# A fused decoder block on Trainium2: column halves and a narrow inverse root in the first cross-attention

## What is computed

```python
q = einsum('oc,bcn->bon', Wq, x);  k, v = split(einsum('oc,bcn->bon', Wkv, context), 2)
q = softmax(split_heads(q), axis=-2) * scale     # over the 64 channels of a head
k = softmax(split_heads(k), axis=-1)             # over the 512 positions
ctx = einsum('bhdn,bhen->bhde', k, v)
out = einsum('bhde,bhdn->bhen', ctx, q)
out = einsum('oc,bcn->bon', Wout, out) + b_out
return (out - mean(out, 1)) * rsqrt(var(out, 1) + 1e-05) * g
x = layernorm(x + <that>)
```

## Time and profile before

| | us |
|---|---|
| median of 3 runs | 2332.91 |
| lowest, highest | 2332.28, 2333.55 |
| the profiled execution's own time | 2332.89 |
| its span, first to last instruction | 2331.0 |
| PE busy in the span | 2224.3 (95%) |
| DVE busy | 1300.0 (56%) |
| ACT busy | 781.4 (34%) |
| POOL busy | 772.1 (33%) |
| xattn0 on PE, first projection to first product of ffn0 | 563.20 to 859.81 |

### The profile page before, as it was taken

How to read it: one execution, slowest core, us unless ns; L and a number is a source line. 1 busy time by engine, 2 the same in 40 slices (tenths; PEclk the granted TensorE clock), 3 DMA queues, 4 the chain that set the end, 5 groups by cost and what they waited for, 6 DMA issues and landing times.

```text
span 2331.0 us, 33907 instructions
## 1 busy us (share of the span) xinstructions
PE 2224.3 (95%) x11762; PEld 1769.8 (76%) x11762; DVE 1300.0 (56%) x2151; ACT 781.4 (34%) x1475; POOL 772.1 (33%) x709
## 2 busy tenths in 40 slices
PE   8999999997999989999899999999989999999978
PEld 6888888885555547887788888888878888887867
DVE  3454444447677733334345444444766767766766
ACT  2233222223677742222233232222333333232321
POOL 4222222202343336344422122221454344434233
PEclk9999999999999999999899999999999999999989
DMA  4212221221000032230222332222222222222120
GB/s 165 72 58 79 81 79 51 68 55 47 12 17 18 14 126 95 86 108 0 86 72 65 82 82 73 55 73 55 70 65 68 61 61 81 63 72 54 32 78 37
DMA packets 120545, 152.41 MB, mean 65 GB/s; under 512 B 16272, under 2 KB 67984, under 8 KB 119952
## 3 DMA queue, kind: packets, MB, share of 16 engines
q1 hardware_dynamic: 120464, 151.33, 22.4%
HBM read 124.02 MB, written 27.26 MB: 65 GB/s over the span
## 4 chain that ended last, share of the span: by engine, by line
PE 80%; issue 7%; DVE 7%; POOL 4%; ACT 2%; DMA 0%; POOLq 0%; DVEq 0%; ACTq 0%; SPq 0%
PE banks L283 20%; PE banks L285 19%; PE banks L284 18%; PE banks L598 7%; PE banks L641 3%; PE banks L1279 3%; PE banks L1263 2%; POOL f_wl L1690 1%; PE banks L1245 1%; PE banks L1252 1%; PE banks L1215 1%; PE banks L1231 1%; POOL f_il L1698 1%; DVE st L351 1%; PE banks L1269 1%
## 5 line engine op out<-in xcount | busy, mean ns | idle before, releaser
L283 PE MATMUL banks<-xTh,wh 128*128 128x512 f32 x1024 | 418.5, 409 | 11.7 <-DVE xTl L1965 7.5
L285 PE MATMUL banks<-xTh,wl 128*128 128x512 f32 x1024 | 404.3, 395 | 0.0
L284 PE MATMUL banks<-xTl,wh 128*128 128x512 f32 x1024 | 403.2, 394 | 0.0
L283 PE MATMUL banks<-woh,oth 128*128 128x512 f32 x768 | 313.5, 408 | 16.3 <-DVE X L936 7.0
L284 PE MATMUL banks<-wol,oth 128*128 128x512 f32 x768 | 301.8, 393 | 0.0
L285 PE MATMUL banks<-woh,otl 128*128 128x512 f32 x768 | 301.7, 393 | 0.0
L1031 POOL TENSOR_TENSOR sc_sb<-sc_sb,rs 128x512 f32<-128x512 f32 x96 | 103.7, 1083 | 553.2 <-DVE rs L890 553.2
L936 DVE TENSOR_TENSOR X<-banks,X 128x512 f32<-128x512 f32 x192 | 132.0, 688 | 272.9 <-PE banks L285 272.0
L733 ACT ACTIVATE q_sb<-banks 128x512 f32<-128x512 f32 x192 | 114.6, 597 | 402.0 <-PE banks L285 402.0
L283 PEld LDWEIGHTS banks<-xTh,wh 128*128 128x128 f32 x1024 | 195.2, 191 | 52.5 <-issue 9.3
L285 PEld LDWEIGHTS banks<-xTh,wl 128*128 128x128 f32 x1024 | 194.6, 190 | 43.6
(11 more groups left out here) (214 smaller groups left out, 4010.6 us busy)
## 6 DMA issues: line engine op xcount, KB each, us to landing
raw<-in_a_in SPq DMA_DIRECT2D x144, 256.0 KB, 2.8
raw<-in_a_out SPq DMA_DIRECT2D x96, 256.0 KB, 2.8
turned<-pq SPq DMA_DIRECT2D x384, 64.0 KB, 1.8
pt<-turned SPq DMA_DIRECT2D x96, 256.0 KB, 2.8
f_q<-in_f_q SPq DMA_DIRECT2D x21, 512.0 KB, 3.8
f_s<-in_f_s SPq DMA_DIRECT2D x21, 512.0 KB, 5.3
X<-in_x SPq DMA_DIRECT2D x1, 2048.0 KB, 10.7
x_craw<-in_ctx SPq DMA_DIRECT2D x8, 256.0 KB, 2.7
```

The lines of the kernel that those rows point to most:

```text
L283: nc.tensor.matmul(out, w_hi, x_hi, start=start, stop=False)
L284: nc.tensor.matmul(out, w_hi, x_lo, start=False, stop=False)
L285: return nc.tensor.matmul(out, w_lo, x_hi, start=False, stop=stop)
```

## The change

In words:

- `G0` does both batches: 8 products, batch b into partitions 64b to 64b+63 of bank `gm`, that is with weights in column half b of the array, the two batches alternating. `G1` is gone; one `gt` of 128x512 takes the place of two of 64x512. `M0` and `M1` read rows 0 to 63 and 64 to 127 of `x_gt` and of `x_u`, which the setup computes for both halves (16 products for 8). `M1` waits for `m0`.
- `x_m` has no zeros any more: 64 columns per batch. `OUT0` does both batches, 8 products of 128x64 weights, batch b into partitions 64b on, alternating. `OUT1` and the zeroing of `x_m` are gone.
- `VAR` has the squares as weights and two columns of `x_blk` as the moving operand: 4 products of 128x128 by 2 columns, whose 8 results per partition lie in bank `out`. DVE adds epsilon (`ve`, 128x8), POOL raises to -1/2 (`pw`, 128x8), and `BR` on PE spreads the result back over 128x512 of bank `out`: 8 products with 64 equal weight columns and the identity, 128 columns, moving, in column halves. `y` reads that bank. `ln`, `rd` and their two table loads are gone.
- The high part of the context (`ch` on ACT) becomes `chi` on POOL.
- All four orders are new. `OUT` now waits for `y` of the tile before.
- PE's first half of ffn0 stands behind the last `BR`; ACT's high parts stand behind `qc7` and `oc` of tile 7. POOL's hook is the same text, behind `cp` of tile 6.

```diff
-            x_u = sb("x_u", [64, XH * S])
+            x_u = sb("x_u", [P, XH * S])
...
-            x_gt = sb("x_gt", [64, 2, 512])
-            x_m = sb("x_m", [P, 4, 2, P])
+            x_gt = sb("x_gt", [P, 512])
+            x_m = sb("x_m", [P, 4, 2, S])
-            x_sd = sb("x_sd", [P, DM])
-            x_rd = sb("x_rd", [P, DM])
+            x_ve = sb("x_ve", [P, 8])
+            x_r8 = sb("x_r8", [P, 8])
...
-        X_PE = x_order("QT0' K3' KT2' M1'' Q3' KT3' QT1' OUT1'' KT4' XT''' QT2' KT5' Q0 QT3' KT6' VAR'' K0 KT7' "
-                     "QT4' Q1 G0' Q2 QT5' M0' KT0 K1 QT6' G1' QT7' KT1 K2 OUT0' ")
-        X_DVE = x_order("qs0' kn0' qm1' kz'' qs1' y''' m0'' kn1' sm0' bn''' qm2' kn2' xn''' qs2' sm1' kn3' m1'' "
-                     "qm3' qs3' sm2' sm3' xl''' qm0 ")
-        X_ACT = x_order("gt1'' qe1' kc1' qc7'' ke4' ke5' qe2' qc0' kc2' ke6' ke7' ch xhi kc3' qe3' qc1' kc4' "
-                     "xh''' qc2' kc5' sq'' qc3' kc6' ln'' qc4' oc'' kc7' rd'' gt0' ke0 ke1 qc5' qe0 qc6' ke2 "
-                     "kc0 ke3 ")
-        X_POOL = x_order("xl2 cl en4' en5' en6' en7' r'' en0 rs'' en1 en2 cp'' en3 ")
+        X_PE = x_order("Q2' KT2' OUT0'' KT3' K3' QT0' Q3' KT4' QT1' VAR'' XT''' KT5' QT2' Q0 KT6' QT3' K0 KT7' "
+                     "QT4' Q1 G0' QT5' KT0 K1 M0' QT6' BR'' KT1 M1' QT7' K2 ")
+        X_DVE = x_order("sm1' y''' m1'' kn2' qm2' qs2' bn''' sm2' kn3' xn''' qm3' qs3' xl''' ve'' qm0 qs0 kn0 kz' "
+                     "sm3' qm1 sm0 qs1 kn1 m0' ")
+        X_ACT = x_order("ke1 gt0' qc5' kc0 qe1 qc6' ke2 ke3 kc1 qc7' kc2 ke4 ke5 qe2 oc' sq' kc3 qc0 xhi+ ke6 kc4 "
+                     "qc1 xh'' kc5 qc2 ke7 kc6 qc3 qe3 kc7 qe0+ qc4 ke0+ ")
+        X_POOL = x_order("en7' en0 en1 r'' cp''' en2 rs'' en3 chi+ xl2+ cl+ en4 en5 pw' en6 ")
...
-                last = nc.tensor.matmul(pb[h % 2][0:64, (h // 2) * S:(h // 2 + 1) * S], x_wv[r0:r0 + 64, h // 2, :],
-                                        x_woc[r0:r0 + 64, h // 2, :], start=True, stop=True)
+                for c0 in (0, 64):
+                    last = nc.tensor.matmul(pb[h % 2][c0:c0 + 64, (h // 2) * S:(h // 2 + 1) * S],
+                                            x_wv[r0:r0 + 64, h // 2, :], x_woc[r0:r0 + 64, h // 2, :], start=True, stop=True)
...
                 elif kind == "G":
-                    wait(pe, xs["ekt"], 8 * q + 7 + u)
-                    wait(pe, xs[f"ctin{u}"], 16 * (q + 1))
+                    wait(pe, xs["ekt"], 8 * q + 8)
+                    for b in range(2):
+                        wait(pe, xs[f"ctin{b}"], 16 * (q + 1))
+                    wait(pe, xt_ready, q - 1)
+                    for n in range(4):
+                        for b in range(2):
+                            last = nc.tensor.matmul(XB["gm"][64 * b:64 * b + 64, :], x_ct[:, b, n, :], x_ekT[:, b, n, :],
+                                                    start=n == 0, stop=n == 3)
+                    last.then_inc(xs["g"], 1)
+                elif kind == "M":
                     if u == 0:
-                        wait(pe, xs["sd"], q)
+                        wait(pe, xs["gt"], q + 1)
                     else:
                         wait(pe, xs["mr"], 2 * q + 1)
+                    r = slice(64 * u, 64 * u + 64)
                     for n in range(4):
-                        last = nc.tensor.matmul(XB["gm"][0:64, :], x_ct[:, u, n, :], x_ekT[:, u, n, :],
-                                                start=n == 0, stop=n == 3)
-                    last.then_inc(xs["g"], 1)
-                elif kind == "M":
-                    wait(pe, xs["gt"], 2 * q + u + 1)
-                    for n in range(4):
-                        last = nc.tensor.matmul(XB["gm"][:, n * P:(n + 1) * P], x_gt[0:64, u, n * P:(n + 1) * P],
-                                                x_u[0:64, n * P:(n + 1) * P], start=True, stop=True)
+                        last = nc.tensor.matmul(XB["gm"][:, n * P:(n + 1) * P], x_gt[r, n * P:(n + 1) * P],
+                                                x_u[r, n * P:(n + 1) * P], start=True, stop=True)
                     last.then_inc(xs["m"], 1)
                 elif kind == "OUT":
-                    wait(pe, xs["mr"], 2 * q + u + 1)
-                    wait(pe, xs["qcp"], 8 * q + 7 + u)
-                    if u == 0:
-                        wait(pe, xs["osq"], q)
-                        wait(pe, xs["oc"], q)
+                    wait(pe, xs["mr"], 2 * q + 2)
+                    wait(pe, xs["qcp"], 8 * q + 8)
+                    wait(pe, xs["y"], q)
                     for n in range(4):
-                        last = nc.tensor.matmul(XB["out"][:, :], x_m[:, n, u, :], x_q[:, u, n, :],
-                                                start=(u == 0 and n == 0), stop=(u == 1 and n == 3))
+                        for b in range(2):
+                            last = nc.tensor.matmul(XB["out"][64 * b:64 * b + 64, :], x_m[:, n, b, :], x_q[:, b, n, :],
+                                                    start=n == 0, stop=n == 3)
                     last.then_inc(xs["out"], 1)
                 elif kind == "VAR":
                     wait(pe, xs["osq"], q + 1)
-                    wait(pe, xs["mr"], 2 * q + 2)
-                    wait(pe, xt_ready, q)
-                    nc.tensor.matmul(XB["gm"][:, :], x_blk[:, :], x_sq[:, :], start=True, stop=True).then_inc(xs["var"], 1)
+                    wait(pe, xs["oc"], q + 1)
+                    for n in range(4):
+                        last = nc.tensor.matmul(XB["out"][:, 2 * n:2 * n + 2], x_sq[:, n * P:(n + 1) * P],
+                                                x_blk[:, :].rearrange("p (b s) -> p b s", b=2)[:, :, 0], start=True, stop=True)
+                    last.then_inc(xs["var"], 1)
+                elif kind == "BR":
+                    wait(pe, xs["pw"], q + 1)
+                    for n in range(4):
+                        for b in range(2):
+                            last = nc.tensor.matmul(XB["out"][64 * b:64 * b + 64, n * P:(n + 1) * P],
+                                                    x_r8[:, 2 * n + b:2 * n + b + 1].to_broadcast([P, S]), ident[:, :],
+                                                    start=True, stop=True)
+                    last.then_inc(xs["br"], 1)
...
-                if kind == "VAR" and q == NT - 1:
+                if kind == "BR" and q == NT - 1:
                     pe_ffn0(pe, True)
...
-                if kind == "ch" and not (isinstance(q, int) and q == 0):
-                    wait(act, xs["cin"], 16 * (q + 1))
-                    wait(act, xs["k"], 8 * q)
-                    nc.scalar.activation(x_ch[:, :], x_craw[:, :], ACT.Copy).then_inc(xs["chi"], 1)
...
                 elif kind == "gt":
-                    wait(act, xs["g"], 2 * q + u + 1)
-                    wait(act, xs["m"], 2 * (q - 1) + u + 1)
-                    nc.scalar.activation(x_gt[0:64, u, :], XB["gm"][0:64, :], ACT.Copy).then_inc(xs["gt"], 1)
+                    wait(act, xs["g"], q + 1)
+                    wait(act, xs["m"], 2 * q)
+                    nc.scalar.activation(x_gt[:, :], XB["gm"][:, :], ACT.Copy).then_inc(xs["gt"], 1)
...
-                elif kind == "ln":
-                    wait(act, xs["var"], q + 1)
-                    wait(act, xs["rd"], q)
-                    nc.scalar.activation(x_sd[:, :], XB["gm"][:, :], ACT.Ln, bias=x_eps[:, 0:1]).then_inc(xs["sd"], 1)
-                elif kind == "rd":
-                    wait(act, xs["sd"], q + 1)
-                    wait(act, xs["y"], q)
-                    nc.scalar.activation(x_rd[:, :], x_sd[:, :], ACT.Exp, scale=-0.5).then_inc(xs["rd"], 1)
...
-                if kind == "gt" and u == 1 and q == NT - 1:
+                if kind == "qc" and u == 7 and q == NT - 1:
                     high_weight(act, 0, 0)
                     high_weight(act, 0, 1)
-                elif kind == "rd" and q == NT - 1:
+                elif kind == "oc" and q == NT - 1:
                     high_weight(act, 0, 2)
...
-                    wait(dve, xs["out"], 2 * (q - 1) + u + 1)
+                    wait(dve, xs["out"], q)
                     bank = XB["gm"][:, :].rearrange("p (h o) -> p h o", h=4)
                     for h in range(2):
                         r = slice(64 * h, 64 * h + 64)
                         last = nc.vector.scalar_tensor_tensor(
-                            x_m[r, :, u, 64 * u:64 * u + 64], bank[r, :, 64 * h:64 * h + 64], XD ** -0.5,
+                            x_m[r, :, u, :], bank[r, :, 64 * h:64 * h + 64], XD ** -0.5,
                             x_krz[r, 4 * u:4 * u + 4].rearrange("p (h o) -> p h o", o=1).to_broadcast([64, 4, S]),
                             ALU.mult, ALU.mult)
                     last.then_inc(xs["mr"], 1)
+                elif kind == "ve":
+                    wait(dve, xs["var"], q + 1)
+                    wait(dve, xs["pw"], q)
```

(16 more changed lines are left out.)

30 lines of the change are left out of this document (13 added, 17 removed).

## The result

The changed kernel takes **2281.56 us** (median; 2280.18 to 2284.13) beside 2333.23 for the kernel before: ratio 0.9779, with a 95% interval from 0.9762 to 0.9796. That is 51.7 us less; the prediction said 36.5 less. The median lies 0.4 under the low end of the range of 2282 to 2313, and two of the four runs lie inside it. The profiled execution took 2280.18, its span 2278.4. The stage is read from the first query product of xattn0 to the transposes of tile 7, the last thing that ffn0's second half waits for: 307.94 us before (563.20 to 871.14), 257.03 after (561.62 to 818.65), so 50.9 of the 52.7 between the two profiled executions. Of the rest, 1.6 is attn0, which the change does not touch and whose end lies between 560.8 and 564.9 in the runs of this case.

The account below looks back on a forecast made before the run. PE's work was taken to bound the stage. Six periods 30.4, the seventh 5.9 and the start 3, less 0.3 for the setup and 2.5 for the end, gave 36.5 off 2332.9: 2296 us, range 2282 to 2313.

Parts of the forecast that it names:

- Rival A: In `G` and `OUT`, column halves don't run side by side, PE's tile is 34.8: 2347 us, slower; chance 5%.
- Rival B: On PE, weight loads of one half can't run beside the other's products, 4.4 a tile: 2331 us; chance 3%.
- PE per tile, 27.3: In xattn0, PE's work per tile falls from 33.06 to 27.3 us by new prices of `G`, `OUT`, `VAR`, `BR`.
- The period of 28.0: One tile in mid-stage of xattn0 takes 28.0 us instead of 33.06, range 27.3 to 29.5.
- I add 0.7: In the mid-stage period, 0.7 us on PE's 27.3, as PE and DVE with equal turns don't both stay full.
- my round: Walk once round the new order from `qm0`: DVE's waits sum to 2.4 us, its turn to 27.2, as long as PE's.
- case D: In xattn0, overlap is full and the walks have slack: period 27.3, start 6 less, end level, 2286 us; chance 15%.
- `K1` ahead of `Q2`: 3 less: At the stage's start, DVE's wait of 4.39 for `K1` shrinks by the new order: 3 us less, between 0 and 6.
- The seventh period, 5.9: The seventh tile of xattn0, without a next tile's projections, goes from 31.85 to about 26 us: 5.9 less.
- 2.5 more than before: From `G` of tile 7 to ffn0, new work and PE's lower clock make 31.3 us instead of 28.8.
- Rival C: In mid-stage, hand-overs between PE and DVE bind: period 30.5 instead of 28.0, 20 us less gain, 2314 us; chance 12%.
- Five activations: ACT loses five activations (`ln`, `rd`, `ch`, one `gt`) of 0.6 to 0.7 us, besides two table loads of 1.28.

Follow-up runs that it names:

- e7: Changed kernel with both batches' `G` and `OUT` products in one column half, one after the other, the second batch added into the first's place: 2335.9 us, ratio 1.0013.
- e2: Changed kernel with the variance as one 128x512 product and its root by two ACT functions, without `ve`, `pw` and `BR`: 2282.06 us, ratio 0.9791.
- e5: Changed kernel with, in tile 0 alone, the third query pair again ahead of the fourth unit's key transposes and `K1`: 2287.15 us, ratio 0.9801.
- e3: Changed kernel with ffn0's first two low weight parts on POOL behind `rs` of tile 6 instead of `cp`: 2277.94 us, ratio 0.9768.
- e6: As e2, with ACT's second root function behind the last key copies, `y` behind both `M` copies, low parts as in e3: 2270.78 us, ratio 0.9736.
- e11: As e10, with tile 7's variance ahead of tile 6's transposes, `rd` between query copies, `x_xn` ahead of later scalings and `f_wl`: 2272.03 us, ratio 0.9731.
- e10: As e6, with drain orders of its own on PE, DVE and ACT, and ffn0's later scalings spread over tile 6's layer norm: 2276.48 us, ratio 0.9762.
- e12: As e6, another drain: ffn0's first unit behind tile 7's variance, its second behind tile 6's transposes, ACT, DVE and POOL reordered: 2267.42 us, ratio 0.9722.

## Why the prediction was right or wrong

**What bounds the stage, and that the halves run side by side: right.** The forecast rested on `G` and `OUT` falling from 7.16 and 7.07 to 3.7 each. They measured 3.59 and 3.58, and e7 shows that nothing else makes the difference. Rival A (no overlap) falls with it. e7 comes near to what it described and took 2336 instead of the 2347 that I gave it: A priced `BR` at 1.8, while e7 keeps `BR` in column halves at 1.02, and it had the start at 3 instead of 8.5. Rival B falls too: loads of one half are hidden beside products of the other. By the rule of the Trainium skill ("TensorE: Matmul & The Clock Gate", Part 3, The mechanism), a weight load overlaps a running product only if its row group differs. The trace disagrees: with all of the rows in use by both halves, 16 records with 16 loads take 3.59, 0.224 each, while a load alone is 0.14 and a record 0.43 to 0.45.

**PE per tile, 27.3: right within 0.4.** `G` 3.59, `OUT` 3.58, `VAR` 0.82, `BR` 1.02 sum with the old rest to 26.9, as the window shows (26.93). Each of the four prices was 0.08 to 0.12 too high. `BR` at 1.02 lay between its two bounds, 0.6 and 1.8.

**The period of 28.0: wrong, and the largest part of the miss.** The step that failed is "I add 0.7": two engines with equal turns that don't both stay full. In my round DVE's turn came out at 27.2, as long as PE's. Measured, DVE was busy 24.35 and its waits fitted into the 2.6 that were left, so that PE waited for nothing in the middle of the stage. Each wait on the walk was one of DVE, for PE or for ACT, and none was one of PE; a wait of the other engine costs PE nothing as long as the next thing that PE needs is ready. The chance that I should have read from my own walk is case D. e2 shows the other case: 0.29 and 0.62 of waits of PE for ACT and 0.20 for DVE, and there the period was 1.1 over PE's sum. What counts is which engine does the waiting. The miss of 1.07 a period, 0.7 for this term and 0.37 for the prices, is 6.4 us in six; 1.0 more came from the first period, which is 25.9.

**The start: right cause, size too small.** "`K1` ahead of `Q2`: 3 less" measured 3.6 by e5, by the very wait that was named. But the start lost 8.5. The failed step is a term of the sum that was too small: nothing but this one wait was in it. What the new DVE order does in tile 0 besides (its last softmax goes behind the first `G`) was left out, and so was PE's granted clock there, 0.73 before and 0.82 after. Which of them makes the other 4.9 stays open. The range of 0 to 6 was too narrow by it.

**The seventh period, 5.9, and the setup: right.** Measured 5.8. The setup's 32 records take 0.62, as its 16 did: they run in column halves beside each other and cost nothing, instead of 0.3.

**The end: mechanism right in its links, size nearly.** Predicted were `pw` at 1.65 (1.65), an idle PE of 5.8 behind the last `BR` ended by `f_wl` (5.04, `f_wl`), and 2.5 more than before. Up to ffn0's first product it became 0.9 shorter (27.97 against 28.83), and 2.1 of the lower clock fell into ffn0's first half, 13.46 instead of 11.33; both together 1.3 longer. e3 confirms the named culprit: with the low parts one POOL step earlier the stage is 5.8 shorter.

**The range.** 36.5 became 51.7: 7.5 from the periods, 5.5 from the start, 1.2 from the end, 0.3 from the setup, the rest attn0 and what the runs differ by. Rival D named the first of these, and gave 2286; with the start as it measured, it gives 2283. The low end of 2282 was D with a little room for the prices. The period fell under D's, the start by more than D allowed, and the end alone was worse than D's "level"; together they passed the low end by 0.4 us.

**Slips that changed nothing.** Rival C's own sum, 2296 and 8 x 2.5, gives 2316 and not 2314. "Five activations" less on ACT are four, as its own list has them, and the measured 5.2 us less is what two table loads and four activations make. The chain before is not of PE products alone: at 626 us it has one copy by ACT, a wait of 0.40.

## What to carry to other kernels

An engine that reads 100% busy is at its limit only for the instructions it is given: ask how many of the array's rows and columns each of them uses. The Trainium skill ("Perfetto Trace Analysis", Identifying the Most-Contended Engine) says that the busy share of matmuls is not a good measure of how close a kernel is to its limit, and names the arithmetic done against the peak and the busy share of weight loads instead. The trace agrees with the first: PE was 100% busy in both kernels. Its loads went from 18.27 of 33.06 us (55%) to 17.01 of 26.93 (63%), which moves the right way but doesn't tell by itself how much could go.

When two engines have turns of nearly equal length, list the waits by who waits. Here the waits of the second engine, 2.6 a tile, were free, and waits of the one that binds were the cost. Placing one function of ACT behind three others instead of ahead, with one swap on DVE, took a tile from 27.04 to 26.50, under the 26.93 of a whole new path over GpSimd.

The orders of the steady state were not right for the last tile here. Of three orders for the drain alone, tried one by one, two went wrong by a wait that moved; what helped was to ask what the next stage really needs, and to send everything else behind it.

## What the runs showed of the hardware that I had not expected

- Float32 products in two column halves overlap completely: 16 records of 512 moving columns in 3.58 to 3.59 us against 7.01 in one half, although both stream out of the same 128 partitions.
- The overlap doesn't need strict alternation. One by one 3.58, in blocks of two products (four records) 3.63, in blocks of four products 5.35. In these runs the other half was taken up about four records ahead.
- The lower clock struck different places of nearly equal drains: the last `OUT` took 3.65 in e6 and e11, 5.98 in e10 and 5.35 in e12, where the granted clock of the window from 782 to 786 was 0.59. PE had been busy 3.48 of 4.00 us just before in e12 and 3.53 of 4.00 in e6. What tips it was not settled.
- `x_xn`, a DVE operation on 128x512, took 2.56 in e6 while POOL ran `f_wl`, and 0.53 to 0.55 in mid-stage; with `f_wl` moved behind it (e11) it took 0.55 in the drain too.
